# Four-layer transformer kernel on one core: loads split and reordered, a bias row sent from ScalarE's queue, and the steps ahead of the expert loop placed anew

## The reference

```python
x = x + tanh(g_xattn[0]) * L0_xattn(layernorm(x), ctx, ctx)   # 2 heads, attn = softmax0 - lam*softmax1, rms norm
x = x + tanh(g_ffn[0])   * L0_ffn(layernorm(x))               # router: softmax, top-p 0.8; 8 experts:
#   h = relu(x @ W1[e] + b1[e]);  y = h @ W2[e] + b2[e];  sum over e of gate[e] * y
x = x + tanh(g_xattn[1]) * L1_xattn(layernorm(x), ctx, mask)  # 16 heads, products of Wq, Wk, Wv, Wo
x = x + tanh(g_ffn[1])   * L1_ffn(layernorm(x))               # fake-quantised gate, up, down
```

## Time and profile before

| | |
|---|---|
| median of 3 runs | 178.59 us (178.3 to 179.68) |
| the profiled execution | 179.74 us |
| its span, first to last instruction | 178.0 us |
| PE busy | 163.3 us (92%), 890 instructions |
| DVE busy | 133.1 us (75%) |
| ACT busy | 100.9 us (57%) |
| POOL busy | 59.6 us (34%) |
| mean granted TensorE clock | 0.965 |

### The profile page before, as it was taken

How to read it: one execution, slowest core, us unless ns; L and a number is a source line. 1 busy time by engine, 2 the same in 40 slices (tenths; PEclk the granted TensorE clock), 3 DMA queues, 4 the chain that set the end, 5 groups by cost and what they waited for, 6 DMA issues and landing times.

```text
span 178.0 us, 2721 instructions
## 1 busy us (share of the span) xinstructions
PE 163.3 (92%) x890; PEld 132.3 (74%) x890; DVE 133.1 (75%) x322; ACT 100.9 (57%) x283; POOL 59.6 (34%) x72
## 2 busy tenths in 40 slices
PE   6999899999999998999999999999999987879861
PEld 6787887768876866788878867788888876749850
DVE  2577878994677688975978688969855379569893
ACT  2357688668947828595853659993526200345130
POOL 3224578567258886060001242110420213000100
PEclk9999999999999999999999999999999999569985
DMA  5798217442964610100005301021010000000003
GB/s 160 201 299 322 105 43 268 176 96 93 270 206 168 234 62 4 59 0 2 2 4 146 93 0 59 0 63 61 0 59 0 4 0 2 0 0 4 0 0 118
DMA packets 8409, 15.04 MB, mean 84 GB/s; under 512 B 1560, under 2 KB 3768, under 8 KB 8139
## 3 DMA queue, kind: packets, MB, share of 16 engines
q1 hardware_dynamic: 7962, 14.64, 26.0%
q10 hardware_dynamic: 432, 0.23, 0.5%
...
## 4 chain that ended last, share of the span: by engine, by line
PE 51%; DVE 26%; ACT 8%; DMA 6%; issue 4%; POOL 2%; SPq 1%; DVEq 0%; ACTq 0%; POOLq 0%
PE ps L712 46%; DVE hlo L1297 5%; PE ps L709 5%; DMA raw<-in_experts 4%; ACT hhi L626 3%; DVE xn L1117 2%; DVE l1w L1430 2%; DVE hmx L1424 2%; DVE stats L1107 1%; DVE kvo L1459 1%; DMA xs<-in_x 1%; POOL rstd L358 1%; ACT raw L496 1%; ACT xn L484 1%; DVE dif L1192 1%
## 5 line engine op out<-in xcount | busy, mean ns | idle before, releaser
L1297 DVE SCALAR_TENSOR_TENSOR hlo<-ps,hhi 128x512 fp32r<-128x512 f32 x64 | 43.8, 686 | 24.8 <-ACT hhi L626 24.4
L626 ACT ACTIVATE hhi<-ps 128x512 fp32r<-128x512 f32 x64 | 37.9, 597 | 31.2 <-PE ps L712 31.1
L712 PE MATMUL ps<-xhi,w1hi 128*128 128x512 f32 x64 | 30.3, 473 | 0.9 <-DVE hlo L1297 0.7
L712 PE MATMUL ps<-hhi,w2hi 128*128 128x512 f32 x64 | 25.3, 396 | 0.6 <-DVE hlo L1297 0.5
L712 PE MATMUL ps<-hlo,w2hi 128*128 128x512 f32 x64 | 25.4, 396 | 0.0
L712 PE MATMUL ps<-hhi,w2lo 128*128 128x512 f32 x64 | 25.3, 395 | 0.0
L712 PE MATMUL ps<-xhi,w1lo 128*128 128x512 f32 x64 | 25.2, 393 | 0.0
L712 PE MATMUL ps<-xlo,w1hi 128*128 128x512 f32 x64 | 25.1, 392 | 0.0
L358 POOL TENSOR_TENSOR rstd<-ve,mhalf 128x2 f32<-128x2 f32 (+1 forms) x12 | 8.9, 738 | 43.0 <-DVE ve L1112 43.0
L712 PE MATMUL ps<-ident 128*128 128x64 f32 x134 | 18.6, 296 | 2.1 <-POOL ident L384 1.7
L712 PEld LDWEIGHTS ps<-ident 128*128 128x128 f32 x134 | 18.4, 215 | 2.9 <-POOL ident L384 1.7
...
## 6 DMA issues: line engine op xcount, KB each, us to landing
...
```

The lines of the kernel that those rows point to most:

```text
L626: eng.activation(hhi[:, n % 4, :], ps[:, UPB[n % 3], :], ACT.Relu).then_inc(s["hi_ready"], 1)
L712: return eng.matmul(dst, lhsT, rhs, start=start, stop=stop)
L1297: eng.scalar_tensor_tensor(hlo[:, n % 4, :], ps[:, UPB[n % 3], :], 0.0, hhi[:, n % 4, :].bitcast(F32), ALU.max, ALU.subtract).then_inc(s[" ...
```

## The change

SP's loads are split and sent in another order: of expert 0 W1 comes ahead of W2 in a DMA of its own (with a semaphore of its own for W2), the `l1w` block comes in four parts with four semaphores, keys first and ahead of W2 of expert 0. The 512-element DMA for b1's first row leaves SP's queue and goes to ScalarE's, behind the first evacuation. The store of `b1_dram` moves from SP to ScalarE too. On ScalarE, POOL, TensorE and VectorE the steps ahead of the loop stand in another order; `wt_evac(1)` moves from ScalarE to VectorE; POOL gets three waits (`fold_rows(0)` for `xn_ready` 2, `low1(0)` for `w_ready` 2, `fold_rows(2)` for `xnb_ready`). Work and results stay the same; 5 of the small `ident` products that keep TensorE running go and 2 come.

```diff
@@ names @@
-            raw_loaded0 raw_loaded1 b1_loaded wr0_loaded ...
+            raw_loaded0 raw_loaded1 w2_loaded l1wk_loaded l1wo_loaded b1_loaded wr0_loaded ...
@@ SP @@
-            load_expert(0)
-            b1_0 = late_at["b1T"][0]
-            eng.dma_start(vot_row[:, 0:F].rearrange("a (f p) -> a f p", p=P),
-                          late[:, b1_0:b1_0 + FT].rearrange("p (a f) -> a f p", a=1), allow_slow_non_contiguous=True).then_inc(
-                              s["b1_loaded"], 16)
-            eng.dma_start(l1w[:, 0:2 * INNER], l1w_in[:, 0:2 * INNER]).then_inc(s["l1wa_loaded"], 16)
+            eng.dma_start(w1r[:, 0, :], experts[0, 0:1, 0:F].broadcast_to([P, F])).then_inc(s["raw_loaded0"], 16)
+            eng.dma_start(raw[:, 0, 0:F], experts[0, :, 0:F]).then_inc(s["raw_loaded0"], 16)
+            eng.dma_start(l1w[:, INNER:2 * INNER], l1w_in[:, INNER:2 * INNER]).then_inc(s["l1wk_loaded"], 16)
+            eng.dma_start(raw[:, 0, F:], experts[0, :, F:]).then_inc(s["w2_loaded"], 16)
+            eng.dma_start(l1w[:, 0:INNER], l1w_in[:, 0:INNER]).then_inc(s["l1wa_loaded"], 16)
             eng.dma_start(xs[:, 4:5, :], xv[:, 0, 2:3, :]).then_inc(s["x_loaded2"], 16)
...
+            eng.dma_start(l1w[:, 2 * INNER:3 * INNER], l1w_in[:, 2 * INNER:3 * INNER]).then_inc(s["l1wb_loaded"], 16)
             load_expert(1)
...
-            eng.dma_start(l1w[:, 2 * INNER:], l1w_in[:, 2 * INNER:]).then_inc(s["l1wb_loaded"], 16)
-            eng.wait_ge(s["b1_evac"], 1)
-            eng.dma_start(b1_dram, b1rows[:]).then_inc(s["b1_stored"], 16)
+            eng.dma_start(l1w[:, 3 * INNER:], l1w_in[:, 3 * INNER:]).then_inc(s["l1wo_loaded"], 16)
@@ POOL @@
             inv_root(2, 2, 4)
+            eng.wait_ge(s["xn_ready"], 2)
             fold_rows(0)
+            eng.wait_ge(s["w_ready"], 2)
             low1(0)
...
             for e in range(2, E):
+                if e == 2:
+                    eng.wait_ge(s["xnb_ready"], 1)
                 fold_rows(e)
@@ ACT @@
             eng.activation(kv0T[:, 0, :], ps[:, 7, 0:B * S], ACT.Copy).then_inc(s["kv0_evac"], 1)
+            b1_0 = late_at["b1T"][0]
+            eng.dma_start(vot_row[:, 0:F].rearrange("a (f p) -> a f p", p=P),
+                          late[:, b1_0:b1_0 + FT].rearrange("p (a f) -> a f p", a=1), allow_slow_non_contiguous=True).then_inc(
+                              s["b1_loaded"], 16)
...
+            eng.wait_ge(s["w2_loaded"], 16)
             high2(0)
...
@@ PE @@
-            eng.wait_ge(s["late_loaded"], 16)
-            tr(ps[0:E * FT, 2, 2 * P:3 * P], b1T).then_inc(s["b1t_ready"], 1)
-            eng.wait_ge(s["b1_evac"], 1)
-            keep_running(3, 2)
+            prep_keys(0)
             weights_transposed(0)
-            prep_keys(0)
+            prep_keys(1)
             eng.wait_ge(s["vv_evac"], 1)
             attend(0)
...
@@ DVE @@
+            def wt_evac(c):
+                eng.wait_ge(s["wt_ready"], c + 1)
+                eng.tensor_copy(wT[:, 2 * c:2 * c + 2, :].rearrange("p t d -> p (t d)"), ps[0:S, c, 0:2 * P]).then_inc(
+                    s["wt_evac_d"], 1)
...
+            nlam_step = step(eng.tensor_scalar(nlam[:], nlam[:], LAMBDA_INIT, None, ALU.subtract))
+            row_max(0)
+            eng.wait_ge(s["xt_ready"], 2)
...
+            weights(0, 1)
+            wt_evac(0)
+            prep_evac(0)
+            weights(1)
+            wt_evac(1)
             residual1(0)
```

More of the change, by code:

```diff
@@ L594, in _ @@
             exps(0)
-            eng.wait_ge(s["b1t_ready"], 1)
-            eng.activation(b1rows[:], ps[0:E * FT, 2, 2 * P:3 * P], ACT.Copy).then_inc(s["b1_evac"], 1)
+            place_b1(0)
+            high1(0)
             exps(1)
@@ L602, in _ @@
             eng.activation(VV[:, :, 1, :], vvp[:, :, 1, :], ACT.Copy, scale=tgli[0:S, :]).then_inc(s["vv_evac"], 1)
-            place_b1(0)
-            high1(0)
+            eng.wait_ge(s["w2_loaded"], 16)
             high2(0)
+            prep_evac(1)
             squares(0)
-            wt_evac(1)
+            prep_evac(2)
+            eng.wait_ge(s["b1t_ready"], 1)
+            eng.activation(b1rows[:], ps[0:E * FT, 2, 2 * P:3 * P], ACT.Copy).then_inc(s["b1_evac"], 1)
+            eng.wait_ge(s["b1_evac"], 1)
+            eng.dma_start(b1_dram, b1rows[:]).then_inc(s["b1_stored"], 16)
             squares(1)
-            prep_evac(1)
-            prep_evac(2)
             prep_evac(N_A)
@@ L615, in _ @@
             high_input(0)
+            prep_evac(N_VT)
             high_input(1)
-            prep_evac(N_VT)
             input_copy(0)
@@ L748, in attend @@
             def attend(c):
-                if c == 0:
-                    eng.wait_ge(s["wt_evac_d"], 1)
+                if c < 2:
+                    eng.wait_ge(s["wt_evac_d"], c + 1)
                 else:
-                    eng.wait_ge(s["wt_evac"], c)
+                    eng.wait_ge(s["wt_evac"], c - 1)
                 for j in range(2):
@@ L796, in prep_pair @@
                 if u < N_VT:
+                    eng.wait_ge(s["l1wa_loaded"], 16)
                     eng.wait_ge(s["pevac_a"], on_act(N_A - 1))
                 if u == N_A + 2:
-                    eng.wait_ge(s["wt_evac"], 1)
+                    eng.wait_ge(s["wt_evac_d"], 2)
                 if u in (N_A2, N_VOT + 2, N_VOT + 4):
@@ L802, in prep_pair @@
                 if u == N_VOT:
+                    eng.wait_ge(s["l1wo_loaded"], 16)
                     eng.wait_ge(s["pevac_a"], on_act(u - 1))
@@ L926, in _ @@
             weights_transposed(1)
-            prep_keys(1)
+            eng.wait_ge(s["late_loaded"], 16)
+            tr(ps[0:E * FT, 2, 2 * P:3 * P], b1T).then_inc(s["b1t_ready"], 1)
+            prep_keys(2)
             attend(1)
-            prep_keys(2)
-            keep_running(2, 2)
             prep_pair(N_A)
@@ L933, in _ @@
             prep_values(N_VT)
+            prep_values(N_VT + 1)
             keep_running(1, 2)
@@ L937, in _ @@
             input_transposes(1)
-            prep_values(N_VT + 1)
+            keep_running(2, 3)
             def up(n):
@@ L1143, in row_max, with weights @@
                                   ALU.max, negate=True).then_inc(s["nmx0_ready"], 1)
-            def weights(c):
+            def wt_evac(c):
+                eng.wait_ge(s["wt_ready"], c + 1)
+                eng.tensor_copy(wT[:, 2 * c:2 * c + 2, :].rearrange("p t d -> p (t d)"), ps[0:S, c, 0:2 * P]).then_inc(
+                    s["wt_evac_d"], 1)
+            def weights(c, between=None):
                 t0 = CH_T0[c]
@@ L1150, in weights @@
                 ev = E0[:, t0:t0 + 2, :, :].rearrange("p t h s -> p (t h) s")
-                after(step(eng.tensor_tensor(ev, ev, rc0[:, 2 * t0:2 * t0 + 4].unsqueeze(2).broadcast_to([P, 4, S]), ALU.mult)))
+                n = step(eng.tensor_tensor(ev, ev, rc0[:, 2 * t0:2 * t0 + 4].unsqueeze(2).broadcast_to([P, 4, S]), ALU.mult))
+                if between is not None:
+                    row_max(between)
+                after(n)
                 eng.scalar_tensor_tensor(Wt[:, t0:t0 + 2, :], E0[:, t0:t0 + 2, 1, :], nlam[:],
@@ L1264, in _ @@
             normalise(2, 2, 4).then_inc(s["xn_ready"], 1)
-            eng.wait_ge(s["xt_ready"], 2)
-            eng.tensor_copy(xT[:, 256:512], ps[:, 1, 0:256]).then_inc(s["xt_evac_d"], 1)
-            row_max(0)
             eng.wait_ge(s["tanh_ready"], 1)
@@ L1271, in _ @@
             after(step(eng.tensor_tensor(nlam[:], lam_e[:, 1:2], lam_e[:, 0:1], ALU.subtract)))
-            after(step(eng.tensor_scalar(nlam[:], nlam[:], LAMBDA_INIT, None, ALU.subtract)))
-            row_max(1)
-            weights(0)
-            eng.wait_ge(s["wt_ready"], 1)
-            eng.tensor_copy(wT[:, 0:2, :].rearrange("p t d -> p (t d)"), ps[0:S, 0, 0:2 * P]).then_inc(s["wt_evac_d"], 1)
-            weights(1)
-            prep_evac(0)
+            nlam_step = step(eng.tensor_scalar(nlam[:], nlam[:], LAMBDA_INIT, None, ALU.subtract))
+            row_max(0)
+            eng.wait_ge(s["xt_ready"], 2)
+            eng.tensor_copy(xT[:, 256:512], ps[:, 1, 0:256]).then_inc(s["xt_evac_d"], 1)
             eng.tensor_scalar(sig127[:], gth[:, 4:6], 0.5 / QMAX, 0.5 / QMAX, ALU.mult, ALU.add)
             tbo_step = step(eng.tensor_scalar(tbo[:], bo_bc, gth[:, 1:2], None, ALU.mult))
+            after(nlam_step)
+            weights(0, 1)
[3 more added lines that the diff above has]
+            wt_evac(1)
             residual1(0)
```

6 lines of the change are left out of this document (3 added, 3 removed).

## The result

The changed kernel takes **189.68 us** (median of 4 executions, 189.11 to 192.15), the kernel before on the same chip 178.8 (178.3 to 179.68): a ratio of 1.059, 95% interval 1.052 to 1.066. It is 6% slower. The forecast was 177.8 us with a range of 176.2 to 180.0. In what follows a median is over all executions of a kernel, and a ratio leaves the disturbed ones out; the profiled execution of a1, a2, b1, b4, c1, c3 and d2 is one of the slower of its kernel, that of b3 and c2 one of the fastest.

A forecast was written before the change was run, and what follows sets the result against it. TensorE was taken as the limit, with the loop's start moving the end. From the profiled 179.74, less 0.44 and 0.4, came 178.9; for the median, 178.59 - 0.84 = 177.75, say 177.8 us, range 176.2 to 180.0.

The forecast's parts named there:

- What bounds the kernel: TensorE over the whole run: the loop's start moves the end equally; better feeding gives at most some 1.9 us more.
- Part 1: Exponentials ahead of the loop: row_max(0) moved forward, exps(0) start 0.78 us sooner at 9.42; the moved DMA issue costs nothing.
- Part 2: Ahead of the loop, low1(0) hangs on w_ready 2: starts at 15.17 against 15.61, 0.44 us sooner; tail 8.77 us.
- Part 3: SP's reordered loads: fold_rows(0) can start at 8.4 to 9.2, worth at least nothing; keys taken as landed by 12.08.
- Part 4: fold_rows(2) waits for xnb_ready, so VectorE's normalisations of steps 2 and 3 run unblocked: 0 to 0.7, taken 0.4 us gained.
- rival 1: POOL's later work meets the router's last small steps; gates up to 1.1 us later, 179.2 us; chance 0.22.
- Rival 2: b1's first row lands late, 10.3 to 16.2, stopping ScalarE at place_b1(0); up to 182.7 us; chance 0.13.
- Rival 3: Gates and expert 5's load come sooner and TensorE's waits up to 72 us shrink: 1.3 us more, 176.4; chance 0.18.
- Rival 4: The granted clock falls to half for 6.9 us at the loop's start, costing 3.4 us: 181.2; chance 0.05.

The follow-up runs named there:

- a1: The changed kernel with the DMA of b1's first row back on SP, behind expert 0's W2: 183.05 us, ratio 1.014 to the kernel before.
- a2: The kernel before with only the DMA of b1's first row moved from SP to ScalarE's queue: 186.4 us, ratio 1.040.
- b1: a4 without the wait of fold_rows(2) for xnb_ready: 180.58 us, ratio 1.005 to the kernel before.
- b4: b1 with place_b1(0) and high1(0) put back behind exps(1) and VV on ScalarE: 181.03 us, ratio 1.011 to the kernel before.
- c1: The changed kernel with b1's first row as one 2 KB piece on SP, behind expert 0's W2: 179.88 us, ratio 1.004 to the kernel before.
- c3: b3 with Part 1 alone, row_max(0) ahead of chunk 1's copy on VectorE: 179.46 us, ratio 1.002 to the kernel before.
- d2: b3 with prep_values(N_VT + 1) ahead of the inputs' transposes and keep_running(2, 3) behind them: 179.4 us, ratio 1.002 to the kernel before.
- b3: The kernel before with b1's first row as one 2 KB piece at its old place on SP: 178.87 us, ratio 1.000.
- c2: c1 without the wait of fold_rows(2) for xnb_ready: 179.35 us, ratio 1.002 to the kernel before.
- a4: The changed kernel with b1's first row read as one 2 KB piece, still on ScalarE's queue: 180.22 us, ratio 1.005 to the kernel before.
- a3: The changed kernel with SP holding its loads behind expert 0's W2 until b1's first row has landed: 181.05 us, ratio 1.011 to the kernel before.
- d1: c2 with prep_values(N_VT + 1) back behind the inputs' transposes in place of keep_running(2, 3): 179.24 us, ratio 1.000 to the kernel before.
- b2: a4 without the wait of low1(0) for w_ready: 180.06 us, ratio 1.006 to the kernel before.

## Why the prediction was wrong, by its own steps

**What bounds the kernel**: right. The end moved with the loop's start, 9.37 for 9.70 us. (The waits that the view of the earlier trace rows names add up to 1.7 us, not 1.9.)

**Part 1.** The issue was "taken for nothing" at 0.54 to 0.78 us. It took 1.26 and held the first evacuation until 7.16 instead of 6.19, and `exps(0)` started at 9.86 instead of 9.42. With the row in one piece the issue took 0.52 and `exps(0)` started at 9.43 (a4). So the moves were counted rightly, but the price of a DMA of 512 elements was read from another queue at another time. The 0.78 us are of no use at the end: c3 didn't gain by them, and in a4 ScalarE, early by them, waits 0.99 us for the fold.

**Part 2.** Without the row in the way `low1(0)` starts at 14.93 to 15.48 (c2, a4; forecast 15.17), and the tail from there to the start is 23.69 - 14.93 = 8.76 us (forecast 8.77). The tail was right; that the 15.17 fits is luck. It was built on `place_b1(0)` at 10.65 with 1 us of cover behind it. There was no such cover: `place_b1(0)` came at 11.19 to 11.75, held by the fold, and `low1(0)` followed 3.73 us behind it in every trace that has the wait. "0.44 us sooner" failed besides because it was made against one trace, in which TensorE was slow until 11.9. b3, with the old placement and TensorE fast earlier, starts at 23.70, the new placement at 23.69. No gain is seen.

**Part 3**: wrong, its first sentence ahead of all. `fold_rows(0)` started at 10.96, not at 8.4 to 9.2, and "Lower bound of its worth: nothing" was wrong too, since its end is what `place_b1(0)`, and with it the start, hangs on once the row is in time. SP's stall was no loss: it held the following loads back while W1 went through. With W1 in a load of its own (256 KB) the fold started at 9.22 with SP held (a3), and at 9.85, 10.30, 10.45 and 10.96 without (c1, d1, a4, the changed kernel); with W1 and W2 in one load (512 KB) at 9.77 behind the stall, and at 10.86, 10.98 and 11.28 without it (b3, d2, c3). What is let in is not all of it: a1, whose SP stood still until 10.86, folded at 9.92, no sooner than c1, and c1 and d1 differ by 0.45 with the same loads. The keys were not "landed": TensorE waited 0.75 us for them, 0.60 in a4.

**Part 4**: the first half is right. The normalisations of step 2 took 0.59 us for two in place of 1.58. The blocking went to the gates' last steps, as rival 1 said. In place of a gain of 0.4 there is a loss of 0.4: 14.63 or 14.64 us from start to gates in a4, b2, a3 and the changed kernel, 14.24 to 14.26 in b1, b3, c2, c3 and before. The rule of the Trainium skill ("SBUF — State Buffer", "SBUF: two separate sides") quoted for rival 1 agrees with the two steps of 0.19 us that took 1.17 and 1.18, until a POOL operation had ended. It is not the 1.1 us of the rival, since the unblocked normalisation and comparison won most of it back.

**Rival 2** is what happened, and the forecast failed there, at "I take the lower end, because the row ... has a queue of its own now". The move to that queue is what made it late (a2: with nothing else moved, the row lands at 19.31 and the loop starts 7.3 us later). The landing, 19.48, also lies beyond the upper bound of 16.2. That bound was the longest life that the row could have had on SP, where only expert 0's load was ahead of it; on the other queue it shared the engines with all of SP's loads. By the rival's own price, 1 us for each us beyond 12.1, 19.48 gives 178.59 + 7.4 = 186.0. What it lacked is the clock: from `raw<-VOT` to the start it is 34.08 - 19.57 = 14.51 us, against 12.50 in a4, so 2.0 more by the half clock. With 12.50 us from there on, the start of before (24.38) answers to `place_b1(0)` at 11.88; 19.57 is 7.7 us beyond it, and 7.7 and 2.0 are the 9.70 by which the start moved. The 0.4 us of the gates don't show at the end of this execution: the load of expert 5 lands at 60.97 for 51.25, 9.72 later. The medians, 189.68 and 178.8, are 1.5 us further apart than the two profiled executions, and these 1.5 are not located.

**Rival 3** didn't occur. **Rival 4** did in kind, though not at its place: the clock fell while TensorE waited 8 us, at some 17 us. At the place that it named, the loop's start, it fell in b4 and c1, for 6 us, about its 6.9. I had given it 0.05, and b1, b4 and c1 all show a fall, b1's from 17 to 23 us.
